# Attention scores issued half a unit ahead and gated tiles moved to the head of their place, in a fused eight-layer transformer kernel

## The reference

```python
x = x + _L1_ffn_ref(_layernorm(x), ...)           # 8-bit fake-quantised gated feed-forward, 352 hidden
x = x + _L2_xattn_ref(_layernorm(x), ctx, ...)    # 16 heads of 8
x = x + _L2_ffn_ref(_layernorm(x), ...)           # "slots": top 8 of 64, GRU-like update, read back
x = x + _L3_xattn_ref(_layernorm(x), ctx, ...)    # 16 heads of 64
x = x + _L3_ffn_ref(_layernorm(x), ...)           # shared expert + top 2 of 8 experts
```

```python
scale = sigmoid(clip) * max(abs(x)) / 127
xq = clip(round(x / scale), -128, 127) * scale    # the maximum is over the whole tensor
h = silu(xq @ w_gate.T) * (xq @ w_up.T)           # then h is quantised in the same way and multiplied with w_down
```

## Time and profile before

| what | value |
|---|---|
| runs | 2337.83, 2343.54, 2347.81 us |
| the profiled execution | 2347.68 us, its span 2345.9 us |
| PE busy (matmul) | 1911.0 us, 81% |
| DVE busy | 1507.8 us, 64% |
| ACT busy | 1292.4 us, 55% |
| POOL busy | 630.4 us, 27% |
| granted TensorE clock, mean of the span | 0.907 of full speed |

### The profile page before, as it was taken

One profiled execution on the slowest core, in us unless ns is written; L12 is line 12 of the kernel. 1 busy time (PEld: TensorE's weight loads), 2 busy tenths in 40 slices (PEclk: granted clock), 3 DMA queues, 4 the chain that ended last, 5 costly groups with the idle time before them and its releaser, 6 DMA issues.

```text
span 2345.9 us, 49910 instructions
## 1 busy us (share of the span) xinstructions
PE 1911.0 (81%) x17542; PEld 1551.2 (66%) x17544; DVE 1507.8 (64%) x3920; ACT 1292.4 (55%) x4431; POOL 630.4 (27%) x626
## 2 busy tenths in 40 slices
PE   3987998888899984477888889888989888888774
PEld 2776877777787772256566667777767766666663
DVE  5987776777778985555655755656556464645342
ACT  2765655556566664355676656565556544544421
POOL 0003031422211300132333332442433413232421
PEclk9988999999999996577899998997989999999987
DMA  7002444443543002100000112211212222222253
GB/s 221 29 15 94 123 142 141 127 137 118 153 136 104 29 6 106 54 18 10 23 1 19 37 29 76 77 58 59 74 53 72 67 71 77 76 76 82 86 155 109
DMA packets 125126, 184.21 MB, mean 79 GB/s; under 512 B 10320, under 2 KB 82064, under 8 KB 124624
## 3 DMA queue, kind: packets, MB, share of 16 engines
q1 hardware_dynamic: 116688, 164.23, 23.0%
q0 software_dynamic: 8192, 16.79, 2.3%
HBM read 145.52 MB, written 35.45 MB: 77 GB/s over the span
## 4 chain that ended last, share of the span: by engine, by line
PE 35%; DVE 10%; ACT 6%; issue 6%; POOL 1%; DMA 1%; SPq 0%; DVEq 0%; ACTq 0%; POOLq 0%
PE ps L1614 6%; PE ps L1863 4%; ACT pb L2003 4%; PE ps L1842 3%; PE ps L1849 3%; PE ps L1652 3%; PE ps L1636 2%; PE ps L1643 2%; DVE nm L2355 2%; PE ps L1625 2%; PE ps L1821 2%; PE ps L1670 1%; DVE hT L2146 1%; ACT pt L2011 1%; DVE hT L2141 1%
## 5 line engine op out<-in xcount | busy, mean ns | idle before, releaser
L2003 ACT ACTIVATE pb<-ps,nm 128x128 f32<-128x128 f32 x1024 | 363.3, 377 | 264.2 <-DVE nm L2355 264.0
L2044 POOL TENSOR_TENSOR pb<-pb,rcs 128x512 f32<-128x512 f32 x256 | 266.7, 1042 | 803.3 <-DVE rcs L2344 802.3
L968 ACT ACTIVATE pb<-pb,nm 128x128 f32<-128x128 f32 x1024 | 313.0, 392 | 81.7 <-DVE nm L1191 81.7
L2355 DVE TENSOR_REDUCE nm<-ps 128x8 f32<-128x1024 f32 x128 | 156.0, 1219 | 139.3 <-PE ps L1849 72.1
L2364 DVE COPY pt<-ps 128x512 f32<-128x512 f32 x128 | 88.3, 690 | 220.0 <-PE ps L1863 220.0
L2003 ACT ACTIVATION_READ_ACCUMULATOR pb<-ps,nm 128x1 f32 x1024 | 222.0, 217 | 0.0
L1863 PE MATMUL ps<-w,pb 128*128 128x128 f32 x1024 | 174.2, 297 | 49.2 <-ACT pt L2011 42.9
L1614 PE MATMUL ps<-hT,big 128*128 128x128 f32 x960 | 151.4, 308 | 58.7 <-DVE hT L2146 42.6
L1614 PEld LDWEIGHTS ps<-hT,big 128*128 128x128 f32 x960 | 134.9, 216 | 83.8 <-DVE hT L2146 58.1
L1863 PEld LDWEIGHTS ps<-w,pb 128*128 128x128 f32 x1024 | 128.3, 153 | 79.8 <-issue 66.6
L1191 DVE TENSOR_REDUCE nm<-pb 128x8 f32<-128x1024 f32 x128 | 156.1, 1220 | 4.4
(11 more groups left out here) (367 smaller groups left out, 4419.7 us busy)
## 6 DMA issues: line engine op xcount, KB each, us to landing
big<-in_we SPq DMA_DIRECT2D x92, 514.0 KB, 3.6
big<-in_we SPq DMA_DIRECT2D x120, 384.0 KB, 3.1
big<-sorted_in SPq DMA_DIRECT2D x8, 960.0 KB, 6.1
sorted_out<-big SPq DMA_DIRECT2D x28, 256.0 KB
sorted_in<-big SPq DMA_DIRECT2D x4, 1472.0 KB, 12.1
sorted_out<-h_all SPq DMA_DIRECT2D x16, 256.0 KB
hidden<-h_all SPq DMA_DIRECT2D x7, 512.0 KB, 2.9
h_all<-hidden SPq DMA_DIRECT2D x7, 512.0 KB, 3.7
```

What stands on the lines that cost most here:

```text
L968: m = a.activation(pb[:, n % 2, k * S:(k + 1) * S], pb[:, n % 2, k * S:(k + 1) * S], ACT.Exp, bias=nm[:, n % 2, k:k + 1])
L2003: m = a.activation(pb[:, n % 2, e * S:(e + 1) * S], ps[:, score_bank(n) + half, k * S:(k + 1) * S], ACT.Exp, bias=nm[:, n % 2, e:e + 1], a ...
L2044: g_.tensor_tensor(p4, p4, r4.unsqueeze(2).to_broadcast([P, 4, S]), ALU.mult).then_inc(n2["p_normed"], 1)
L2355: v.tensor_reduce(nm[:, n % 2, :], ps[:, bank:bank + 2, :].rearrange("p a (j k) -> p (a j) k", k=S), AX, ALU.max, negate=True).then_inc(n2 ...
```

## The change

In the quantised layer PE gets extra products of the identity matrix with itself, 9 before the first `turn` and 3 after each pair of products, 81 in all. Their results go to the free half of bank 7 and nobody reads them.

```diff
+                def idle_work(count):
+                    for k in range(count):
+                        pe.matmul(ps[:, 7, 256 + k % 2 * P:256 + (k % 2 + 1) * P], ident, ident, start=True, stop=True)
 
                 spread_max(1)
+                idle_work(IDLE_B * NC1)
                 turn(0)
...
                         pe.matmul(ps[0:m, c, :], wgq[:, at:at + m], xqT[j % 2], start=True, stop=True)
                         pe.matmul(ps[0:m, 3 + c, :], wuq[:, at:at + m], xqT[j % 2], start=True, stop=True)\
                             .then_inc(moe["hid_psum"], 1)
+                        idle_work(IDLE_B)
                     if j + 1 < NG:
                         turn(j + 1)
```

```diff
                 for hs in range(FIRST, LAST + 1):
-                    n = unit_at.get(hs)
...
+                    n, follows = unit_at.get(hs), unit_at.get(hs + 1)
+                    if n is not None and n not in alternating:
+                        scores(n)
                     work(0, hs)
                     p = unit_at.get(hs - 1)
                     for half in range(2):
                         if p is not None:
-                            pe.wait_ge(n2["p_normed"], 2 * p + 1 + half)
                             if half:
                                 pe.wait_ge(n2["p_hi"], p + 1)
                             elif p:
                                 pe.wait_ge(n2["p_lo"], p)
+                            pe.wait_ge(n2["p_normed"], 2 * p + 1 + half)
                             for k in range(4):
                                 m = pe.transpose(ps[:, BANK_T, k * S:(k + 1) * S],
                                                  pb[:, p % 2, (4 * half + k) * S:(4 * half + k + 1) * S], ident)
@@ -1866,6 +1876,8 @@
                         if half == 0:
                             values(hs)
                             work(1, hs)
+                            if follows in alternating:
+                                scores(follows)
                     work(2, hs)
```

```diff
                 def work(place, hs):
+                    if place == 1:
+                        for item in evacuations(place, hs):
+                            tile(*item)
...
-                    for item in evacuations(place, hs):
-                        tile(*item)
+                    if place == 2:
+                        for item in evacuations(place, hs):
+                            tile(*item)
```

```diff
                 def work(place, hs):
+                    for item in hidden_rows(place, hs):
+                        tile(*item)
...
-                        if g is not None and place == 2:
+                        if g is not None and place == (1 if number[(2, g, 2 * b)] in alternating else 2):
...
-                    for item in hidden_rows(place, hs):
-                        tile(*item)
-
...
+                    if n in alternating:
+                        maxima(n)
                     if p is not None:
                         sums_inv(p, 1)
+                    if n is not None and n not in alternating:
+                        maxima(n)
                     work(1, hs)
                     if n is not None:
```

More of the change, by code:

```diff
@@ L1207, in build @@
         FF_ORDER = list(range(1, NG)) + [0]
+        IDLE_B = 3
         spread = hT[:, 7, 0:P]
@@ L1824, in values @@
                         m.then_inc(n2["pv"], 1)
-                for hs in range(FIRST, LAST + 1):
-                    n = unit_at.get(hs)
-                    if n is not None:
-                        _, layer, g, t = units[n]
-                        bank = score_bank(n)
-                        if score_bank_free(n):
-                            pe.wait_ge(n2["exps"], 2 * score_bank_free(n))
-                        if layer == 2:
-                            b, c = divmod(t, 2)
-                            if c == 0:
-                                pe.wait_ge(n2["q_ready"], G * g + b + 1)
-                                if g:
-                                    pe.wait_ge(n2["k_col"], g)
-                            for k in range(BLK):
-                                i, a = divmod(k, 2)
-                                at = 32 * (2 * c + a)
-                                m = pe.matmul(ps[:, bank + a, i * S:(i + 1) * S], qm[at:at + 32, i, b * S:(b + 1) * S],
-                                              keys[g % 2][at:at + 32, b * S:(b + 1) * S], start=True, stop=True)
-                        else:
-                            pe.wait_ge(n2["q_col"], IC3 * g + t + 1)
-                            pe.wait_ge(n2["k3_col"], IC3 * g + t + 1)
-                            for b in range(G):
-                                for a in range(2):
-                                    m = pe.matmul(ps[:, bank + a, b * S:(b + 1) * S],
-                                                  q3[t % 2][64 * a:64 * a + 64, b * S:(b + 1) * S],
-                                                  k3[t % 2][64 * a:64 * a + 64, b * S:(b + 1) * S], start=True, stop=True)
-                        m.then_inc(n2["scores"], 1)
@@ new lines, in scores @@
+                def scores(n):
+                    _, layer, g, t = units[n]
+                    bank = score_bank(n)
+                    if score_bank_free(n):
+                        pe.wait_ge(n2["exps"], 2 * score_bank_free(n))
+                    if layer == 2:
+                        b, c = divmod(t, 2)
+                        if c == 0:
+                            pe.wait_ge(n2["q_ready"], G * g + b + 1)
+                            if g:
+                                pe.wait_ge(n2["k_col"], g)
+                        for k in range(BLK):
+                            i, a = divmod(k, 2)
+                            at = 32 * (2 * c + a)
+                            m = pe.matmul(ps[:, bank + a, i * S:(i + 1) * S], qm[at:at + 32, i, b * S:(b + 1) * S],
+                                          keys[g % 2][at:at + 32, b * S:(b + 1) * S], start=True, stop=True)
+                    else:
+                        pe.wait_ge(n2["q_col"], IC3 * g + t + 1)
+                        pe.wait_ge(n2["k3_col"], IC3 * g + t + 1)
+                        for b in range(G):
+                            for a in range(2):
+                                m = pe.matmul(ps[:, bank + a, b * S:(b + 1) * S],
+                                              q3[t % 2][64 * a:64 * a + 64, b * S:(b + 1) * S],
+                                              k3[t % 2][64 * a:64 * a + 64, b * S:(b + 1) * S], start=True, stop=True)
+                    m.then_inc(n2["scores"], 1)
@@ L2332, in work, with maxima @@
                         combine(g)
-                    for item in hidden_rows(place, hs):
-                        tile(*item)
                 def hs_rows():
                     return hs_c[:, :].unsqueeze(1).to_broadcast(both)
+                def maxima(n):
+                    v.wait_ge(n2["scores"], n + 1)
+                    if n >= 2:
+                        v.wait_ge(n2["exps"], 2 * (n - 1))
+                    bank = score_bank(n)
+                    v.tensor_reduce(nm[:, n % 2, :], ps[:, bank:bank + 2, :].rearrange("p a (j k) -> p (a j) k", k=S), AX,
+                                    ALU.max, negate=True).then_inc(n2["maxed"], 1)
                 def sums_inv(n, half):
```

7 lines of the change are left out of this document (removed).

## The result

The changed kernel takes 2240.89 us (median of 4 runs, 2238.61 to 2251.46), the kernel before 2340.68 us beside it on the same chip (4 runs, 2331.56 to 2347.81). The ratio is 0.958, its 95% interval 0.954 to 0.962: some 100 us faster, where 72 were forecast. The profiled execution took 2251.46 us with a span of 2249.7 us; its clock is 0.928, before it was 0.907.

What follows compares the result with a forecast made beforehand. PE is busiest but never full, held by a closed attention loop and waits for bank 6. Terms -35 - 40 + 2 + 1 = -72 us give 2276, or 2272 us at the median; own range 2245 to 2300, whole range 2228 to 2322.

Steps and rivals of the forecast that it cites:

- the tail: Tail stage: DVE puts tiles of group 6 ahead of the last group's norm and router, 2 us lost of 114.
- part 2: Expert stages: tiles at the head of their place cut PE's 80.9 us wait for bank 6; 40 us gained.
- part 1: Attention stages: scores half a unit ahead, maxima and masked queries earlier; 23 + 12 = 35 us gained.
- the pair of units: Regular warm attention pair: maxima start 0.39 and 1.25 us earlier, together 1.64 of 12.10 us; 23 us over 28 units.
- The turns start as before: Regular attention pair: the scores, 1.16 us, fit into PE's pause of 1.38 us, so the turns are not delayed.
- my own sign of it: Warm attention pairs: wrong if the turns' second half starts later than 3.4 us behind the maxima.
- The third rival: Attention stages: at the lower clock moved scores push the turns back 1.9 us per unit; 2366 us, chance 0.07.
- My sign against part 2: Expert stages: wrong if DVE's idle time before a tile, released by ACT's tanh, grows as much as PE's wait falls.
- the fourth rival: First attention and expert stages: filled pauses keep PE at 2.4 GHz, more than the sum; about 2235 us, chance 0.10.
- The fifth rival: DVE and ACT: strictly ordered, some 130 tiles push what follows, 74 us eat the gain; 2340 us, chance 0.05.
- ACT's order: ACT's tile items at the head of place 1 can hold the query copy and second four exponentials; 3 us lost.
- Part 3: Quantised layer: identity products lift the clock near 1, period stays 5.85 us, nothing reaches the next stage; 1 us lost.

Runs made afterwards that it cites:

- the turns put in their place: Changed kernel with PE issuing the turns' first half ahead of place 0's projection product up to the 52nd unit: 2238.09 us, ratio 0.956 to the kernel before.
- the kernel with the tiles alone: Kernel before with only DVE's tile items moved to the head of places 1 and 2: 2372.63 us, ratio 0.969.
- the last group: Changed kernel again, 2246.45 us; with masked queries at place 1 and ACT's tiles at tail, 2227.62; also turns first in half-steps 24 to 42, 2227.83; before 2341.42.

## Why the prediction was right, and where it was off

**The sum.** 72 us less were forecast (2272 us), 100 us less measured (2240.89 us). The direction, the whole range (2228 to 2322 us) and the order of the parts were right. But the gain was 28 us short, and the time lies below the forecast's own range, 2245 to 2300 us. By parts: the scores 24 us in the trace, 25 us alone (35 forecast), the tiles 74 us and 75 us alone (40 forecast), the identity products 0 (1 lost), the tail 3 us gained (2 lost). Against these stand 5 us by which the stretch ahead of the quantised layer happened to be longer in the profiled execution. The term of the sum that was mis-sized most is part 2, 40 us for 75. That the sum isn't further off is in part luck: part 1 was too large by 10 us, part 2 too small by 35.

**Part 1** was right in its mechanism and wrong in how it was spread. The first 24 units gave 20 us where 12 were taken; the following 28 gave 4.5 us where 23 were taken, and the stretch up to the 52nd unit is 360 us, not about 350. The 20 us are uncertain themselves: the eight kernels with the scores ahead take 156.1 to 163.3 us for the first 24 units, the four without 182.8 to 184.3. The step that failed is the pair of units: it was to win 1.64 us and won 0.73, and it was generalised over 28 units. The row that I summed over both stages, DVE's wait for scores, says it when it is cut at unit 24 in the kernel before, first the first stage, then the second:

```profile
DVE nm L2355 <- PE ps L1842: 26.3, 17, 3.2
```

```profile
DVE nm L2355 <- PE ps L1842: 12.7, 11, 1.6
```

Two thirds of the 39.0 us lay in the first stage, and 12.7 us was what DVE waited for these scores in the warm stage. PE's wait for ACT ahead of the turns fell there from 17.5 to 2.8 us, as meant, but its waits for ACT and DVE ahead of products into the projections' bank rose from 0.7 to 13.8 us (L1643 6.6, L1669 4.8, L1659 2.4). "The turns start as before" was wrong, and my own sign of it, more than 3.4 us behind the maxima, came up: 4.07 us. The scores had not stood idle in their old place. They lay between two projection products that use one bank, and covered ACT's and DVE's evacuation of it. That this is the cause is shown by the turns put in their place: they give 0.86 us back, and the pair wins 1.59 us over the kernel before, nearly the 1.64 forecast. Over the 28 units even this order wins only 9 us, so the regular pair doesn't stand for the stage. The third rival, cold turns, did not happen: the first stage has the same clock as before, 0.72, and PE is idle in it for 36.7 instead of 51.9 us. (What I held against that rival, that a PE that waits less was granted more in every later stage, isn't so in the tail of the earlier trace rows: idle for 44% of it, against 27% in the first stage, and granted 0.80.)

**Part 2.** I took 60% of PE's 80.9 us; 62.5 us went, 77%. Of this, new waits took a part: idle time fell by 45 us in the two stages (22.4 + 22.6), which is about my 40. The masked queries, for which I took 6 us and at most 10, cost 7.8 us of waiting. My sign against part 2 didn't come up: DVE's idle time before a tile, released by ACT's tanh, was 9.9 us and is 10.3 us. The missing term is the clock: 29 us of PE's busy time in the changed kernel, 36 us in the kernel with the tiles alone. I had it as the fourth rival for the expert stages at a chance of 0.10, priced it only in the attention stage, and left it out of the sum, though 2.08 us for the eight products stood in the earlier trace rows right behind the pause of 3.68 us.

The time, 2241 us, lies much nearer to that rival's 2235 us than to the forecast, but that is chance. The price came from the first attention stage, whose clock stayed at 0.72. And it doesn't add up: half of 34 us under 2272 us is 2255 us, and even all of it gives 2238.

The fifth rival, tiles that hold what follows on a strictly ordered engine, is refuted as a whole. (The sentence on the page's rule in the prediction calls it the third; the fifth is meant.) As a small effect it is real at the masked queries of 12 sequences. I took 3 us for ACT's order; the runs can't tell it from nothing, and not from some 10 us.

**Part 3** came out at nothing, as said, but two figures on the way were off. PE's clock in the layer rose from 0.50 to 0.82 over the 37 us of the earlier trace rows, not near 1 (0.95 with the identity products alone), and PE was busy for 21.84 us of them, 59%, not over 80%. An identity product takes 0.28 us at the higher level (three in 0.83 us), where I took at most 0.16; nine are 2.5 us, not 1.4. Single products of the layer took 0.38 instead of 0.64 us, and the period stayed, because PE does not set it. The next stage starts at the lower clock as before.

## What to carry to other kernels

Price a pause of the matmul engine twice: by its own length, and by what the instructions behind it take at the lower clock; here, by PE's busy and idle time, the second was as large as the first. Before an operation is moved out of a place, look at what it covers there, above all between two users of one bank, and cut a wait that you put a price on by the stages in which it is to be won. When one step goes to the head of a queue, follow the releases that now stand behind it, and look what they already cost: the masked queries were worth 14.5 us more, and PE had waited 11.2 us for them before the change.

## What the hardware showed that I had not expected

The same eight f32 products took 2.08 us behind a pause of 3.69 us and 1.06 us without it, and the lower clock held on for most of an 18 us unit (0.59) although PE was busy for 15.51 us of it. A stretch that no edit had touched didn't keep its clock: units 0 to 24 took 163.3 us in one kernel and 156.1 us in another with the same instructions there, at 0.73 and 0.80, with PE busy for 131.2 and 122.2 us. A second profile of the changed kernel, taken with the last group, repeated its unit times to 0.1 us in all 127 units. So a few microseconds between two kernels can be the clock's and still repeat. What sets the clock in the first 24 units, and why it held on for 18 us, stays open.
